# Feed-forward stage: V as 64-column weights, probabilities normalised before they are transposed, half of the exps head by head, and a new order on the engines

## The reference

```python
qkv = x @ Wqkv
q = l2norm(q) * qs;  k = l2norm(k) * ksc
q = q * cos * scale + rotate_half(q) * sin * scale
k = k * cos * inv + rotate_half(k) * sin * inv
sim = jnp.einsum('bhwie,bhwje->bhwij', bq, bk2) * QK_SCALE      # 8.0
sim = jnp.where(mask, -jnp.finfo(sim.dtype).max, sim)
attn = jax.nn.softmax(sim, -1)
out = jnp.einsum('bhwij,bhwje->bhwie', attn, bv2)
return out.reshape(b, n, INNER) @ Wo                           # 16 heads of 64
```

## Time and profile before

| | us |
|---|---|
| median of 3 runs | 3237.13 |
| lowest, highest run | 3236.29, 3239.09 |
| span of the profiled execution | 3240.0 |
| busy in it: TensorE, VectorE, GpSimd, ScalarE | 2737.4, 2611.0, 2324.6, 2198.7 |

### The profile page before, as it was taken

How to read it: one execution, slowest core, us unless ns; L and a number is a source line. 1 busy time by engine, 2 the same in 40 slices (tenths; PEclk the granted TensorE clock), 3 DMA queues, 4 the chain that set the end, 5 groups by cost and what they waited for, 6 DMA issues and landing times.

```text
span 3240.0 us, 52326 instructions
## 1 busy us (share of the span) xinstructions
PE 2737.4 (84%) x12731; PEld 1679.3 (52%) x12841; DVE 2611.0 (81%) x7422; ACT 2198.7 (68%) x4098; POOL 2324.6 (72%) x2545
## 2 busy tenths in 40 slices
PE   5878788887888888888888879789999999999997
PEld 2334333343433334343433448657777777777776
DVE  4999999999999999999999973367777777777774
ACT  3777777777777777777777753357676676766765
POOL 6777777777777777777777740087877878777782
PEclk9999999999999999999999988889999999999998
DMA  5333433334333333433333340000010101010000
GB/s 133 72 73 70 78 72 72 72 72 75 70 77 72 72 72 71 77 70 75 72 72 73 70 121 1 1 1 1 0 37 0 37 0 37 0 37 0 0 0 7
DMA packets 368022, 163.09 MB, mean 50 GB/s; under 512 B 285166, under 2 KB 298228, under 8 KB 367220
## 3 DMA queue, kind: packets, MB, share of 16 engines
q1 hardware_dynamic: 367988, 162.65, 23.9%
HBM read 156.81 MB, written 5.80 MB: 50 GB/s over the span
## 4 chain that ended last, share of the span: by engine, by line
PE 40%; DVE 40%; issue 9%; ACT 7%; POOL 2%; DMA 1%; SPq 1%; DVEq 1%; POOLq 0%; ACTq 0%
PE bank L1368 9%; PE bank L1432 5%; PE bank L1613 5%; DVE bank L1065 4%; PE bank L1383 3%; DVE bank L1060 3%; ACT qkv_w L772 3%; PE bank L1691 3%; DVE sq L1040 3%; DVE bank L1040 3%; DVE rot_s L1281 3%; PE bank L1450 3%; DVE fix_trace L1131 2%; DVE ss L1284 2%; PE bank L1473 2%
## 5 line engine op out<-in xcount | busy, mean ns | idle before, releaser
L623 POOL TENSOR_TENSOR kT<-upto,xT 128x512 f32<-128x512 f32 x260 | 270.7, 1041 | 378.8 <-PE bank L1373 378.7
L1065 DVE TENSOR_REDUCE bank<-qkv_w 128x2 f32<-128x768 f32 x512 | 466.0, 955 | 88.5 <-ACT qkv_w L795 64.2
L1368 PE MATMUL bank<-diag_h,w_part 128*128 128x512 f32 x1024 | 374.4, 487 | 161.1 <-DVE bank L1060 161.1
L1065 DVE TENSOR_REDUCE qkv_w<-qkv_w 128x4 f32<-128x1536 f32 x256 | 448.1, 1750 | 47.5 <-ACT qkv_w L788 30.3
L1368 PEld LDWEIGHTS bank<-diag_h,w_part 128*128 128x128 f32 x1024 | 184.5, 190 | 409.7 <-issue 385.9
L709 POOL TENSOR_TENSOR qk<-rot_c,rot_s 128x512 f32<-128x512 f32 x192 | 244.8, 1275 | 207.7 <-DVE rot_s L1281 207.7
L1368 PE MATMUL bank<-diag_x,w_part 128*128 128x512 f32 x1032 | 385.1, 495 | 10.2 <-DMA diag_x<-diag_ring 10.2
L788 ACT COPY qkv_w<-bank 128x512 f32<-128x512 f32 x258 | 221.0, 857 | 249.9 <-PE bank L1368 249.9
L637 POOL TENSOR_TENSOR diag_h<-eye,part 128x512 fp32r<-128x512 f32 x384 | 389.1, 1042 | 0.0
L1383 PE MATMUL bank<-qT,wh 128*128 128x256 f32 (+1 forms) x768 | 255.4, 468 | 152.7 <-DVE qT L1047 151.7
L716 POOL TENSOR_TENSOR rs<-rs,halfs 128x8 f32<-128x8 f32 x192 | 320.4, 1669 | 16.0
(11 more groups left out here) (239 smaller groups left out, 6607.8 us busy)
## 6 DMA issues: line engine op xcount, KB each, us to landing
diag_x<-diag_ring SPq DMA_DIRECT2D x259, 512.0 KB, 6.7
qkv_w<-in_L_ffn_Wqkv SPq DMA_DIRECT2D x6, 1536.0 KB
diag_ring<-X SPq DMA_DIRECT2D x264, 4.0 KB, 5.4
diag_ring<-o_fin SPq DMA_DIRECT2D x8, 512.0 KB, 8.1
o_w<-in_L_ffn_Wo SPq DMA_DIRECT2D x6, 512.0 KB
w<-in_L_ffn_W SPq DMA_DIRECT2D x6, 341.0 KB
b<-in_L_ffn_b SPq DMA_DIRECT2D x6, 341.0 KB
w<-in_L_ffn_W SPq DMA_DIRECT2D x6, 128.0 KB
```

Source lines behind the costliest of these rows:

```text
L623: pool.tensor_tensor(tri[n][:, rows, :], upto[:].unsqueeze(1).to_broadcast([P, 4, D]), src[:, rows].unsqueeze(2).to_broadcast([P, 4, D]), ...
L1065: return dve.tensor_reduce((pre, bias_at[0])[n][:, a:b], chain[n][:, a:b, :], AX_X, ALU.add)
L1368: return pe.matmul(dst, w_part[:, n, w], diag[n][:, d, a:b, :].rearrange("p n k -> p (n k)"), start=False, stop=True, skip_group_check=True)
```

## The change

It changes the feed-forward slots on all four engines.
- The factor 8 of the scores moves into the rotation tables of q.
- V is kept without the column of ones (`v_tok` in place of `v_aug`; the fill of ones goes). `values(c)` takes V of one head as the weights (64 columns) and streams probT (128 columns). Even heads give partitions 0 to 63 of the output, odd ones 64 to 127, so that the attention's output comes out already transposed, in banks 4 and 5. `turn_att` and `att` go; `attended(c)` on ScalarE copies to attT.
- The probabilities are normalised ahead of `probs`. For heads 0 to 7 VectorE subtracts the maximum as before, ScalarE runs one exp over 1024 columns, and VectorE sums it (`denominators`). For heads 8 to 15 ScalarE reads the scores from PSUM, in eight exps of 128 columns with the negated maximum as bias and the sum as a second output. VectorE then takes reciprocals and multiplies, 128x1024 in `prob` by 8 values of `rden`, once for each half.
- The semaphores of paired banks are split in two, and the order is new on TensorE, VectorE, ScalarE and GpSimd. On GpSimd the deviation stands between the third and the fourth chunk, and the addition of b2 after the fourth.

The core of the diff (the same rewriting of the semaphores in the rest, and definitions that only become functions, are left out):

```diff
-        (cos * scale, cos * scale), (sin * scale, -sin * scale),
+        (SCORE_SCALE * cos * scale, SCORE_SCALE * cos * scale), (SCORE_SCALE * sin * scale, -SCORE_SCALE * sin * scale),
...
-            pool.memset(v_aug[:], 1.0)
...
-                    for c in range(4):
-                        chunk(c)
-                if mid:
-                    norm()
+                if new:
+                    rotated(0)
+                    unit_length(0)
+                    scaled(0)
...
+                    scaled(2)
+                if mid:
+                    deviation()
+                if new:
+                    rotated(3)
+                    unit_length(3)
+                    scaled(3)
+                if mid:
+                    add_bias()
...
+                def exp_of_rows():
+                    act.wait_ge(s_sub, i)
+                    act.activation(prob[:, 0:1024], prob[:, 0:1024], ACT.Exp).then_inc(s_exp[0], 1)
+                def exp_of_heads():
+                    act.wait_ge(s_less, i)
+                    for h in range(8):
+                        at = (h % 4) * T
+                        ins = act.activation(prob[:, 1024 + h * T:1024 + (h + 1) * T], bank[:, 2 + h // 4, at:at + T],
+                                             ACT.Exp, bias=less_mx[:, 1, h:h + 1], scale=1.0,
+                                             accum_out=den[:, 1, h:h + 1])
+                    ins.then_inc(s_exp[1], 1)
...
+                def maximum(n, done):
+                    dve.wait_ge(s_ready, two + (n - 1))
+                    dve.tensor_reduce(less_mx[:, n, :], scores, AX_X, ALU.max, negate=True).then_inc(done, 1)
+                def subtract():
+                    dve.wait_ge(s_max, i)
+                    dve.tensor_tensor(rows_of(0), scores, less_mx[:, 0, :].unsqueeze(2).to_broadcast([P, 8, T]),
+                                      ALU.add).then_inc(s_sub, 1)
+                def denominators():
+                    dve.wait_ge(s_exp[0], i)
+                    dve.tensor_reduce(den[:, 0, :], rows_of(0), AX_X, ALU.add).then_inc(s_den, 1)
...
+                def normalise(n):
+                    dve.wait_ge(s_rden[n], i)
+                    dve.tensor_tensor(rows_of(n), rows_of(n),
+                                      rden[:, 8 * n:8 * n + 8].unsqueeze(2).to_broadcast([P, 8, T]),
+                                      ALU.mult).then_inc(p_ready, 1)
...
                 def values(c):
-                    for h in range(a, b):
-                        ins = pe.matmul(bank[:, 6 + c % 2, (h - a) * (FD + 1):(h - a + 1) * (FD + 1)],
-                                        probT[:, h, :], v_aug[:, par, h, :], start=True, stop=True)
-                    ins.then_inc(pv_ready, 1)
+                    for m in range(4):
+                        for odd in (0, 1):
+                            h = 8 * c + 2 * m + odd
+                            ins = pe.matmul(bank[64 * odd:64 * odd + 64, 4 + c, m * T:(m + 1) * T], v_tok[:, par, h, :],
+                                            probT[:, h, :], start=True, stop=True)
+                    ins.then_inc(attT_ready[c], 1)
```

More of the change, by code:

```diff
@@ L950, in slot, with table, gelu, hidden @@
                                    bias=ln_b[:, bass.ds(layer, 1)]).then_inc(xnT_copied, 1)
+                def table(of, n):
+                    act.wait_ge(warm_ready, two + n)
+                    act.activation(warm[:, 1:2], warm[:, 0:1], of).then_inc(warm_ready, 1)
+                def gelu():
+                    act.wait_ge(gate_ready, i - 2)
+                    act.activation(gate_g[:], gate_in[:], ACT.Gelu).then_inc(gelu_ready, 1)
+                def hidden():
+                    act.wait_ge(hgT_ready, i - 2)
+                    act.copy(hgT[:, 0:2, :], heads_of(bank[:, 7, 0:2 * T], 2, T))
+                    act.copy(hgT[0:FI - 256, 2, :], bank[0:FI - 256, 7, 2 * T:3 * T]).then_inc(hgT_copied, 1)
+                if score:
+                    turned(1)
+                    turned(0)
+                if new:
+                    square(0)
+                    square(1)
                 if mid:
@@ L953, in slot @@
                     probs(1)
-                    exp(1, two - 2)
                 if score:
                     turned(2)
+                if old:
+                    normed()
+                table(ACT.Gelu, 1)
+                if score:
                     turned(3)
@@ L961, in slot @@
                     probs(2)
-                    probs(3)
-                if score:
-                    exp(0, two - 1)
                 if new:
                     square(3)
-                act.wait_ge(warm_ready, two + 1)
-                act.activation(warm[:, 1:2], warm[:, 0:1], ACT.Gelu).then_inc(warm_ready, 1)
+                if mid:
+                    probs(3)
+                if old:
+                    gelu()
+                table(ACT.Exp, 2)
+                if score:
+                    exp_of_rows()
+                if mid:
+                    attended(1)
+                if ahead:
+                    bring(i + 1, 1 - par)
+                if mid:
+                    attended(0)
                 if new:
@@ L1345, in slot @@
                                       ALU.mult).then_inc(xn_ready, 1)
+                if new:
+                    rotate(0)
+                    squares(0)
+                    rotate(1)
+                    squares(1)
+                if score:
+                    maximum(0, s_max)
+                    subtract()
+                if old:
+                    gate_bias()
+                    value_bias()
+                if new:
+                    rotate(2)
+                if score:
+                    maximum(1, s_less)
+                if old:
+                    gated()
+                if new:
+                    squares(2)
+                if score:
+                    denominators()
+                if new:
+                    rotate(3)
+                    squares(3)
+                if score:
+                    reciprocals(0)
+                if mid:
+                    add_attended()
+                if score:
+                    normalise(0)
+                if mid:
+                    statistics()
+                if score:
+                    reciprocals(1)
+                if old:
+                    add_hidden()
+                if mid:
+                    norm()
+                if score:
+                    normalise(1)
             slots(dve, UNITS, 4, slot)
@@ L1680, in turn_att @@
-                def turn_att(c):
-                    pe.wait_ge(att_ready, 3 * i - 3)
-                    pe.wait_ge(pT_copied, four + (c - 5))
-                    transposed(bank[:, 4 + c, :], att, 512 * c, 4, attT_ready)
+                    pe.matmul(bank[:, 7 - c, 0:FI], xnT[:], w1_k[:, (1 - c) * FI:(2 - c) * FI],
+                              start=True, stop=True).then_inc(hg_ready, 1)
                 def attention_out():
                     wo_j = o_w[:, bass.ds(place(pe, i - 2)[2], 1)]
-                    pe.wait_ge(attT_copied, two - 2)
+                    for c in range(2):
+                        pe.wait_ge(attT_copied[c], i - 1)
```

276 lines of the change are left out of this document (129 added, 147 removed).

## The result

| | before | after |
|---|---|---|
| median of the runs beside each other, us | 3238.1 | 3090.4 |
| lowest, highest | 3236.3, 3239.3 | 3087.9, 3095.7 |
| span of the profiled execution | 3240.0 | 3088.4 |

The ratio is 0.9544, 95% interval 0.9531 to 0.9558. The kernel is 147.7 us faster; 67 were forecast.

A forecast was written before the change was run, and what follows sets the result against it. TensorE bound the old slot of 22.54 us; GpSimd's floor (20.9) and VectorE's loop (21.5) gave 21.2 for the new. 44 slots gain 59, the ends 8, together 67: 3240.0 - 67 = 3173, 3170.1 against the median; range 3075 to 3240.

The forecast's parts named there:

- The bound: Feed-forward slots: after the change GpSimd bounds, with 18.6 us of its own work and 20.9 with contention.
- TensorE: Feed-forward slot: V's 32 products fall from 3.5 to 2.2 us, all TensorE work from 21.4 to 19.2.
- ScalarE: Heads 8 to 15: eight exps with sums at 0.5 us each, starting 6.6 after the second mask; 18.5 a slot.
- The new cost: Both multiplications of the probabilities and GpSimd's SBUF reads exclude each other for whole instructions, adding 2 x 1.14 us to GpSimd.
- r1 and r2: Waits of VectorE's first and second multiplication for GpSimd's current instruction, each between 0 and the power's 1.67 us.
- the loop through VectorE: Chain from a slot's second mask until the mask may come again: 18.3 us, 19.2 with xn's wait, 21.5 with r1 and r2.
- The race: Second multiplication against GpSimd's power, ready 0.23 and 0.29 after the rotation: slot 20.9 if VectorE wins, 21.5 if not; 21.2 taken.
- Order: The other moves have cover: the deviation ahead of chunk 3 costs nothing, chunk 3 comes about a microsecond before TensorE asks.
- The first rival: Contention does not bite and ScalarE's eight exps decide: slot 18.9 to 19.7 us, total 3086; chance 0.25.
- Column halves: Rival: V's products in column halves do not overlap and cost 3.5 to 3.8 us; total 3210; chance 0.15.
- Exps dearer than 0.75: Rival: exps with a sum above 0.75 us each make it slower; at 0.85 total 3264; chance 0.09, including other mishaps.
- Ends: Both ends of the pipeline, where nothing contends at the draining end, gain 8 us, range 0 to 16.

The follow-up runs named there:

- e5_no_floor: The changed kernel without the lower bound of 1e-24 on the sums of squares, four GpSimd instructions fewer a slot; 3063.2 us, 0.9453 of the kernel before.
- m3_ports_ahead: Pairs of one VectorE multiplication and one GpSimd instruction alone, output a copy of the input, varying what precedes the multiplication; beside an earlier power 1.22 and 1.64 us.
- e7_pool_order: The changed kernel with GpSimd's deviation put back behind chunk 3, as before the change; 3225.6 us, 0.9956 of the kernel before.
- w1_merged: The changed kernel with the head norms of chunks 0 and 1 taken together, one power over 16 columns; 3080.6 us, 0.9524 of the kernel before.
- e1_rden_psum: The changed kernel with the reciprocals of heads 8 to 15 in PSUM instead of SBUF; 3074.3 us, 0.9494 of the kernel before.
- w3_into_power: Reciprocals of heads 8 to 15 in PSUM, plus the first multiplication moved ahead of the addition of the attended half; 3093.3 us, 0.9555 of the kernel before.

## Why the prediction was off

The direction was right and the time lies in the range; the gain is more than twice the forecast, and the slot of 19.43 lies outside the 20.4 to 22.2 by which the prediction said it would be wrong. By its steps:

- **The bound.** GpSimd, as forecast: it waits for nobody in the window, and e5_no_floor confirms it. Its own work is 18.43 (forecast 18.6). Right.
- **TensorE.** V's products 1.90 against 2.2, all work 19.2 against 19.2. Right. The Trainium skill (TensorEngine Tiling (Array Packing), Theoretical Speedup) gives up to twice the speed where a small dimension of up to 64 is tiled by two. The trace agrees: 0.059 a product against 0.118 of the output projection at the same streamed width.
- **VectorE.** 18.0 against 17.8 "if nothing stops it". But 0.8 of the 18.0 is xn being held, so its own work is 17.2, 0.6 less than the sum. Of no consequence here.
- **ScalarE.** An exp with its sum 0.34 against 0.5, start 6.2 after the second mask (2507.43 to 2513.59) against 6.6. Both ends of the bound held; I took a value near the dear one. 16.9 us a slot against 18.5, of no consequence, as ScalarE was off the path.
- **The new cost.** This is the step that failed: "each waited for the other in turn, for the whole instruction", applied to every pair. From it came a floor of 18.6 + 2 x 1.14 and, on the VectorE side, r1 and r2. Measured: one stretch of 1.00 and none for the first multiplication, floor 19.43 instead of 20.9, r1 and r2 both 0. With these, the forecast's own terms give 18.6 + 1.0 = 19.6 for GpSimd and 19.2 for the loop through VectorE, where 21.2 was forecast. The earlier trace rows showed a VectorE subtraction beside casts. The step carried that over to the power. A power lets a multiplication pass once it has run 0.16 us (m3_ports_ahead, 1.22 and 1.64), and powers are 6.7 of GpSimd's 18.4 us; where the multiplication comes first, the power does lose the time (2.67). The product behaves as the earlier trace rows had it, in turn and for the whole instruction: in e7_pool_order the multiplication came 0.13 after it and took 1.99, and GpSimd's next instruction, a rotation, then took 2.25 in place of 1.27.
- **The rule.** The Trainium skill (SBUF — State Buffer, Who interferes with whom) calls the shared port pair an exclusive lock, and says of VectorE's 2-port mode that whoever issues first gets the pair for the whole instruction and the other fully blocks. Of a VectorE instruction with two SBUF inputs it says that it contends with a GpSimd instruction that reads SBUF; the prediction carried "the whole instruction" over to it. For the product the runs agree (1.95 and 1.99), save behind a memset (2.28 for a product that started first). For the power as the first to start, they don't (1.22 and 1.64).
- **The race.** "if VectorE wins, r2 is 0": it won, by 0.06 us, the distance that the forecast's own rows had (0.23 and 0.29). The middle between two cases was taken as one value, which was neither.
- **xn.** +0.8 against +0.9, ending 0.05 after GpSimd's rotation. Right.
- **Order.** The deviation's place was said to cost nothing and was given no gain of its own. e7_pool_order prices it at 135 us, with the clock's 7 in it. Its gain was counted inside the VectorE loop ("from the aggregate to the start of xn 1.22"), but no step said that nearly all of the rest hung on it. That chunk 3 comes "a microsecond before TensorE asks for it" was wrong: TensorE waits 1.0 for it, as it must where GpSimd sets the pace.
- **The first rival.** It gave 3086, next to what came. Its mechanism did not decide: the last sum is there at 2516.49, VectorE takes the reciprocals at 2516.86 without a wait, and then waits 0.84 for the deviation; GpSimd is the bound. Contention did bite, for 1.0 of the forecast 2.3. That the time came out near this rival's is luck.
- **Column halves** (second rival): they overlap. **Exps dearer than 0.75** (third): no.
- **Ends.** 11 against 8.

What stays open: why a power lets a late multiplication pass and a product doesn't, and why a memset directly ahead lets it stop GpSimd. What the swap of V's products and the loss of the transposes of `att` are worth by themselves wasn't seen either, since no kernel puts them back. Of the kernels with all of GpSimd's work none had both multiplications in powers, so what that would give wasn't seen.

## What to carry to other kernels

Price contention by pair of operations and by who starts first, not by engine: list what the neighbour runs at the moment the new instruction comes, and give each case its own time. When four engines stand within a microsecond of each other, a change to one slides the phase and moves the collision, so check a saving by the slot it gives, not by the instruction it shortens (w1_merged saved 0.74 and kept 0.06). In a ring of engines, the place of the smallest instruction in an in-order queue can carry the whole gain: two instructions of 0.8 us here, 135 us.

## Unexpected hardware behaviour

- VectorE's 128x1024 multiplication with both operands in SBUF and GpSimd's power over 8 columns: the power first, 0.16 us or more, neither is held (1.22, 1.64); the multiplication first by 0.06, the power ends 1.52 after it.
- With GpSimd's 128x512 product: whichever starts first holds the other. The product ends 0.90 after the multiplication's end (2.04 in e1_rden_psum, 1.68 in w3_into_power), the multiplication 1.08 after the product's (1.95, 1.99).
- A memset on VectorE directly ahead turns this round: the product and the power are held although they start first (2.28, 2.88).
- GpSimd's power: 1.64 over 8 columns, 2.93 over 16, 10.55 over 64.
- A 128x64 xn with two pointer scalars waits for GpSimd's rotation too: 1.25 against 0.43.
- An exp over 128 columns with a sum is two instructions, 0.37 and 0.2 long, one pair every 0.34.
- TensorE's clock: at half for 3.4 us in every second slot of e7_pool_order, from 2216.36 in the first, where TensorE had done one transpose between 2212.24 and 2215.49. In the slot behind it, with one stop of 1.35 in this place, it stayed full.
- f32 products with 64-column weights: 0.059 each where the halves alternate, 0.078 where they don't.
